# Attention's first chunk of queries and keys loaded in the front stage, into a place of its own

## The reference, cut to what matters

```python
x = x + gnn(layernorm(x), adj)            # 16 heads of 32, adjacency mask
h = rmsnorm(layernorm(x), g1)
q, k, v = split(h @ w_qkv)                # 16 heads of 32; rope on q and k
scores = where(causal, q @ k.T / sqrt(32), -inf)
y = softmax(scores) @ v                   # S = 2048 here
x = x + y @ w_o ; x = x + moe(rmsnorm(x, g2))
```

## Time and profile before

| | us |
|---|---|
| median of 3 runs (lowest, highest) | 2302.75 (2296.74, 2306.21) |
| the profiled execution's own time | 2302.54 |
| span of the profiled execution | 2300.5 |
| what lies around the span | 2.04 |
| front stage, about 702 to 963.1 in the trace | 261 |
| attention stage, 963.1 to about 1735 | 772 |

### The profile page before, as it was taken

How to read it: one execution, slowest core, us unless ns; L and a number is a source line. 1 busy time by engine, 2 the same in 40 slices (tenths; PEclk the granted TensorE clock), 3 DMA queues, 4 the chain that set the end, 5 groups by cost and what they waited for, 6 DMA issues and landing times. The chain is left out here.

```text
span 2300.5 us, 42173 instructions
## 1 busy us (share of the span) xinstructions
PE 2068.8 (90%) x17684; PEld 1222.4 (53%) x17684; DVE 1549.1 (67%) x2552; ACT 1086.7 (47%) x1074; POOL 583.6 (25%) x435
## 2 busy tenths in 40 slices
PE   6899999999995999799999999999991699999997
PEld 3444444444442444344444444444471688888886
DVE  6689999999985567668768777776346544444441
ACT  4778898898971333213444444444420222222221
POOL 2510000000001012414545545544320222222211
PEclk9999999999997999859999999999975799999999
DMA  6421221211215012542030030011030444444421
GB/s 238 147 82 52 73 68 55 73 68 54 74 31 192 37 46 101 162 96 50 19 88 24 24 86 26 20 38 46 24 137 37 170 106 118 120 120 119 119 60 23
DMA packets 86759, 185.33 MB, mean 81 GB/s; under 512 B 13900, under 2 KB 23116, under 8 KB 81036
## 3 DMA queue, kind: packets, MB, share of 16 engines
q1 hardware_dynamic: 77612, 161.68, 21.6%
q0 software_dynamic: 8960, 20.98, 5.0%
HBM read 137.68 MB, written 40.49 MB: 77 GB/s over the span
## 5 line engine op out<-in xcount | busy, mean ns | idle before, releaser
L1406 DVE TENSOR_REDUCE t_rm<-t_m 128x1 f32<-128x512 f32 (+3 forms) x640 | 373.3, 606 | 161.2 <-PE t_m L1527 96.5
L1336 ACT ACTIVATE t_E<-t_s 128x1024 f32<-128x1024 f32 (+3 forms) x320 | 277.3, 895 | 419.8 <-PE t_s L1544 219.4
L1283 POOL TENSOR_TENSOR t_total<-t_E 128x1024 f32<-128x1024 f32 (+2 forms) x151 | 291.8, 1944 | 217.2 <-PE t_d L1571 211.5
L543 ACT ACTIVATE m_step<-m_ub,gat_bias 128x2048 bf16<-128x2048 f32 x128 | 250.0, 1989 | 17.4 <-DMA m_ub<-scratch_uac 12.0
L685 PE MATMUL m_bd<-m_mask,m_S 128*32 128x512 bf16 x3072 | 230.4, 379 | 12.2 <-DVE m_mask L633 12.1
L685 PE MATMUL m_bd<-gat_adjT,m_S 128*32 128x512 bf16 x2496 | 201.4, 379 | 4.9 <-PE m_dn L685 4.9
L685 PE MATMUL m_bd<-m_mask,m_neg 128*32 128x512 bf16 x2496 | 189.0, 379 | 0.0
L1527 PE MATMUL t_m<-tq_K,tq_Q 96*128 96x512 f32 (+2 forms) x320 | 143.7, 477 | 34.4 <-DMA tq_K<-scratch_parts 15.8
L1909 POOL DMA_INDIRECT out<-e_ye,e_token x40 | 80.9, 2024 | 350.9 <-DVE e_ye L2011 341.5
L2075 PE MATMUL e_h<-e_xTh,e_w1h 128*128 128x320 f32 x512 | 159.9, 312 | 3.6 <-PE e_y L2094 2.2
L855 POOL TENSOR_TENSOR o_wq<-o_wq,o_gcol 128x2048 f32<-128x2048 f32 x3 | 11.3, 3807 | 590.3 <-DMA o_wq<-in_L_ffn_w_qkv 590.3
(11 more groups left out here) (317 smaller groups left out, 4126.9 us busy)
## 6 DMA issues: line engine op xcount, KB each, us to landing
a_adj<-in_adj SPq DMA_DIRECT2D x16, 1024.0 KB, 4.9
m_ub<-scratch_uac SPq DMA_DIRECT2D x16, 1024.0 KB, 5.0
e_w1r<-in_L_ffn_w SPq DMA_DIRECT2D x8, 2048.0 KB, 9.4
e_w2r<-in_L_ffn_w SPq DMA_DIRECT2D x8, 2048.0 KB, 9.0
tq_Q<-scratch_parts SPq DMA_DIRECT2D x48, 256.0 KB, 4.9
gat_scale<-scratch_uac SPq DMA_DIRECT2D x32, 256.0 KB
scratch_parts<-o_hi SPq DMA_DIRECT2D x32, 256.0 KB, 2.2
scratch_parts<-o_lo SPq DMA_DIRECT2D x32, 256.0 KB, 2.7
```

The source lines that it names most:

```text
L543: act.activation(step(n), ub[h % 2][:, :].rearrange("p (t q) -> p t q", t=T), ACT.Relu, bias=bias[:, j, h:h + 1], scale=BIG).then_inc(step ...
L1283: pool.tensor_tensor(total[:, two, off:BANK], E[a % 3][:, two, off:BANK], E[(a + 1) % 3][:, two, off:BANK], ALU.add).then_inc(summed[z], 1)
L1336: act.activation(E[n % 3][:, two, off:BANK], ps_s[:, two, off:BANK], ACT.Exp, scale=SCALE).then_inc(exp_done[z], 1)
L1406: dve.tensor_reduce(rm[:, h, t, ch:ch + 1], ps_m[i % 2][:, 0:w], AX, ALU.max).then_inc(entry_read, 1)
```

## The change

Chunk 0 of Q and K of the first four heads gets tensors of its own (`Q0`, `K0`), allocated ahead of the front stage. The front stage's SP loads them (`load_first`) between the stores of qk job 11 and those of job 12, after a wait that three even jobs be stored. The triangles, the block of ones and the ones of K's chunk 0 are made by the front stage's POOL at its start, ahead of `pool.wait_ge(g_in, ...)`. The attention stage drops these instructions and starts SP with chunk 1. The semaphores that count these loads and the setup are the same by name in both stages, with no clearing between them.

For this Q, K, `late_rows` and `late` are now lists of chunks [partition, head, 512], of which chunk 0 is the separate tensor. All accesses are rewritten for that. `load_k` thereby becomes 12 loads of 256 KB where it was three of 1 MB, with rows of 2 KB where they were of 8 KB, in each of its three calls. The ones are written in seven pieces of 2048 in the attention stage where there were two of 8192, and one in the front.

In `ORDER` the v jobs 13, 14 and 15, which stood among the qk jobs 14 to 31, now stand behind the last of them.

```diff
@@ -772,7 +772,7 @@
     ORDER += turns(1) + outs(10, 11) + [qk[3], vs[4]] + outs(11, 12) + [qk[4], vs[5]] + outs(12, 13)
     ORDER += [("var", 2), ("norm", 2), qk[5], vs[6]] + outs(13, 14) + [qk[6], vs[7]] + turns(2) + outs(14, 15)
     ORDER += [qk[7], vs[8]] + outs(15, 16) + [qk[8], vs[9], ("var", 3), ("norm", 3), qk[9], vs[10], qk[10], vs[11]]
-    ORDER += turns(3) + qk[11:14] + [vs[12]] + qk[14:19] + [vs[13]] + qk[19:25] + [vs[14]] + qk[25:] + [vs[15]]
+    ORDER += turns(3) + qk[11:14] + [vs[12]] + qk[14:] + vs[13:]
...
@@ -829,7 +829,17 @@
                 sp.dma_start(C[:, :], cos).then_inc(cs_in, 16)
                 sp.dma_start(S[:, :], sin).then_inc(cs_in, 16)
                 load_x(3)
+
+                def load_first():
+                    sp.wait_ge(sent[0], 32 * 3)
+                    rows = lambda part: parts_dram[part, 0:P, 0:BANK].rearrange("(g d) n -> d g n", g=4)
+                    for stack, order, arrived in ((keep["Q0"], (0, 0, 1), keep["q_in"]), (keep["K0"], (2, 3, 2), keep["k_in"])):
+                        for b, part in enumerate(order):
+                            sp.dma_start(stack[b * DH:(b + 1) * DH, :, :].bitcast(F32), rows(part)).then_inc(arrived, 16)
+
                 for n, (m, g, c) in enumerate(QK):
+                    if n == 12:
+                        load_first()
                     sp.wait_ge(parts_ready, n + 1)
                     for z, part in enumerate((hi, lo)):
                         sp.dma_start(parts_dram[2 * m + z, g * P:(g + 1) * P, c * BANK:(c + 1) * BANK],
@@ -847,6 +857,19 @@
                     pool.tensor_tensor(spun[n % 2][:, :], raw[n % 2][:, :], C[:, c * BANK:(c + 1) * BANK],
                                        ALU.mult).then_inc(cos_done, 1)
...
+
+                triq, trik, ones, setup = (keep[n] for n in ("triq", "trik", "ones", "setup"))
+                pool.memset(triq[:, :], 0.0).then_inc(setup, 1)
+                pool.memset(trik[:, :], 0.0).then_inc(setup, 1)
+                pool.memset(ones[:, :], 1.0).then_inc(setup, 1)
+                pool.wait_ge(setup, 3)
+                pool.affine_select(out=triq[:, :], in_=triq[:, :], compare_op=ALU.is_ge, fill=-1e30,
+                                   base=0, pattern=[[-1, P]], channel_multiplier=1).then_inc(setup, 1)
+                pool.affine_select(out=trik[:, :], in_=trik[:, :], compare_op=ALU.is_ge, fill=-1e30,
+                                   base=0, pattern=[[1, P]], channel_multiplier=-1).then_inc(setup, 1)
+                pool.wait_ge(setup, 5)
+                pool.memset(keep["K0"][ROWS:ROWS + 1, :, :].bitcast(F32), 1.0).then_inc(keep["k_ones"], 1)
+                pool.wait_ge(keep["k_ones"], 1)
 
...
@@ -1092,13 +1115,16 @@
 
 
         with Stage(nc, "tq") as places:
-            Q, K0 = places.sb("Q", [P, G, N], F32R), places.sb("K0", [P, G, N], F32R)
-        late_rows, late = st.sb("rows", [P, G, N]), st.sb("late", [P, G, N])
-        K = [K0, st.sb("K1", [P, G, N], F32R)]
+            Qs, K0s = (places.sb(n, [P, NC - 1, G, BANK], F32R) for n in ("Q", "K0"))
+        rowss, lates = (st.sb(n, [P, NC - 1, G, BANK]) for n in ("rows", "late"))
+        K1s = st.sb("K1", [P, NC, G, BANK], F32R)
+        chunks = lambda first, others: [first[:, :, :]] + [others[:, c, :, :] for c in range(NC - 1)]
+
+        Q, late_rows, late = chunks(keep["Q0"], Qs), chunks(keep["rows0"], rowss), chunks(keep["late0"], lates)
+        K = [chunks(keep["K0"], K0s), [K1s[:, c, :, :] for c in range(NC)]]
...
         E = [st.sb(f"E{i}", [P, G, BANK]) for i in range(3)]
         total = st.sb("total", [P, G, BANK])
-        ones = st.sb("ones", [P, DH])
-        triq, trik = st.sb("triq", [P, P], BF16), st.sb("trik", [P, P], BF16)
+        triq, trik, ones = (keep[n] for n in ("triq", "trik", "ones"))
...
         ve, lg = keep["inv"][:, 1, :], prob
-        W = late[:, 3, :].rearrange("p (k n) -> p k n", k=KD)
-        oT = [late[:, i, :].rearrange("p (k n) -> p k n", k=KD) for i in range(3)]
-        row = lambda t: late_rows[:, t % 4, t // 4 * BANK:(t // 4 + 1) * BANK]
+        W, oT = late[3], late[0:3]
+        row = lambda t: late_rows[t // 4][:, t % 4, :]
...
@@ -1152,25 +1177,27 @@
                 def load_k(q):
                     if q >= 2:
                         sp.wait_ge(s_full[1], (q - 1) * NS)
-                    for b, part in enumerate((2, 3, 2)):
-                        sp.dma_start(K[q % 2][b * DH:(b + 1) * DH, :, :].bitcast(F32), rows(q, part)).then_inc(k_in[q % 2], 16)
+                    for c in range(NC):
+                        for b, part in enumerate((2, 3, 2)):
+                            sp.dma_start(K[q % 2][c][b * DH:(b + 1) * DH].bitcast(F32),
+                                         rows(q, part, slice(c * BANK, (c + 1) * BANK))).then_inc(k_in[q % 2], 16)
 
...
@@ -1201,9 +1228,8 @@
                     for k in range(KD):
                         sp.dma_start(gcol[:, k:k + 1], g2[k * P:(k + 1) * P].rearrange("(p o) -> p o", o=1)).then_inc(g_in, 16)
 
-                for c in range(2):
-                    load_q(0, c)
-                    load_k_first(c)
+                load_q(0, 1)
+                load_k_first(1)
                 maxima(0, 0)
                 for c in range(2, NC):
                     load_q(0, c)
...
@@ -1247,24 +1273,17 @@
                     sp.wait_ge(res_ready, 4 * c + 4)
                     sp.dma_start(rv[:, some, :], X1[:, some, :]).then_inc(res_out, 16)
                     sp.wait_ge(z_ready, 4 * c + 4)
-                    sp.dma_start(zv[:, some, :], late_rows[:, :, c * BANK:(c + 1) * BANK]).then_inc(z_out, 16)
+                    sp.dma_start(zv[:, some, :], late_rows[c]).then_inc(z_out, 16)
...
             @block.gpsimd
             def _(pool):
-                pool.memset(triq[:, :], 0.0).then_inc(setup, 1)
-                pool.memset(trik[:, :], 0.0).then_inc(setup, 1)
-                pool.memset(ones[:, :], 1.0).then_inc(setup, 1)
-                pool.wait_ge(setup, 3)
-                pool.affine_select(out=triq[:, :], in_=triq[:, :], compare_op=ALU.is_ge, fill=BIG,
-                                   base=0, pattern=[[-1, P]], channel_multiplier=1).then_inc(setup, 1)
-                pool.affine_select(out=trik[:, :], in_=trik[:, :], compare_op=ALU.is_ge, fill=BIG,
-                                   base=0, pattern=[[1, P]], channel_multiplier=-1).then_inc(setup, 1)
-                pool.wait_ge(setup, 5)
                 for r in range(2):
-                    pool.memset(K[r][ROWS:K1, :, :].bitcast(F32), 1.0).then_inc(k_ones[r], 1)
-                    pool.wait_ge(k_ones[r], 1)
+                    for c in range(1 - r, NC):
+                        pool.memset(K[r][c][ROWS:K1].bitcast(F32), 1.0).then_inc(k_ones[r], 1)
+                    pool.wait_ge(k_ones[r], NC)
+
                 def add_row(t):
                     pool.wait_ge(y_ready, t + 1)
                     pool.tensor_tensor(X1[:, t, :], X1[:, t, :], row(t), ALU.add).then_inc(res_ready, 1)
...
@@ -1520,12 +1539,12 @@
                         if q == 0:
                             pe.wait_ge(k_first[c], 48)
                         elif c == 0:
-                            pe.wait_ge(k_in[q % 2], 48 * ((q + 1) // 2))
+                            pe.wait_ge(k_in[q % 2], 48 * NC * ((q + 1) // 2))
                     if n >= 2:
                         pe.wait_ge(entry_read, n - 1)
                     diag = ch == c
-                    mm = pe.matmul(ps_m[i % 2][:, 0:w], Q[0:ROWS, h, t * P:(t + 1) * P],
-                                   K[q % 2][0:ROWS, h, ch * BANK:ch * BANK + w], start=True, stop=not diag)
+                    mm = pe.matmul(ps_m[i % 2][:, 0:w], Q[c][0:ROWS, h, t % 4 * P:(t % 4 + 1) * P],
+                                   K[q % 2][ch][0:ROWS, h, 0:w], start=True, stop=not diag)
...
@@ -1536,13 +1555,13 @@
                     if s == BEGIN[c] and z == 0:
                         pe.wait_ge(m_in[c], 64 * (q + 1))
                         if c == 0 and q < 2:
-                            pe.wait_ge(k_ones[q], 1)
+                            pe.wait_ge(k_ones[q], NC)
...
                     for h in (2 * z, 2 * z + 1):
-                        mm = pe.matmul(ps_s[:, h, off:BANK], K[q % 2][0:K1, h, kt * P:(kt + 1) * P],
-                                       Q[0:K1, h, c * BANK + off:(c + 1) * BANK], start=True, stop=not diag)
+                        mm = pe.matmul(ps_s[:, h, off:BANK], K[q % 2][kt // 4][0:K1, h, kt % 4 * P:(kt % 4 + 1) * P],
+                                       Q[c][0:K1, h, off:BANK], start=True, stop=not diag)
...
@@ -2168,6 +2187,14 @@
                     stage_masks(nc, sem, keep, scratch["uac"], scratch["near"], scratch["inv"])
                 recycle()
                 keep["X1"], keep["prob"] = k.sb("X1", [P, T, D]), k.sb("prob", [P, T, EXPERTS])
+
+                with Stage(nc, "first") as first:
```

(12 more changed lines are left out.)

## The result

| | us |
|---|---|
| after, median of 18 runs (lowest, highest) | 2291.11 (2281.67, 2301.77) |
| before, median of 18 runs beside them | 2301.59 (2292.35, 2308.44) |
| ratio after / before, 95% interval | 0.9967 [0.9954, 0.9979] |
| profiled execution: time, span | 2290.23, 2288.5 |

The ratio is 7.6 us in 2301.6 (4.8 to 10.6), the medians differ by 10.5. The forecast was 15.2: half to two thirds of it came. By its interval the gain lies within 0.5%.

What follows compares the result with a forecast made beforehand. PE was taken to bound the kernel, busy 2068.8 of 2300.5 us, with time to win at the seam before attention, where it stood 15.77 us. Terms 4.4 + 10.0 + 0.8 = 15.2 gave 2287.3 us, range 2278 to 2298.

Steps and rivals of the forecast that it cites:

- Part 1: Front stage's end: with the v jobs moved last, the last store lands earlier and attention starts sooner; gain 4.4 us.
- Part 2: Seam to attention: chunk 0 is loaded early, so PE starts 0.2 us after the barrier; gain 10.0 us.
- Part 3: Start of attention: chunk 1's loads arrive without a wait, and some entries run at the upper clock; gain 0.8 us.
- Part 4: Everything behind: later attention moves along unchanged, and POOL's setup and the extra load issues cost 0.
- A: Attention's entries: gain as summed, clock falls soon after they start and rises at the same place of work; 2287.3 us, chance 0.62.
- B: Attention's entries: the clock stays up because PE no longer stands long; 2272.7 us, chance 0.10.
- C: Attention's first quad: the clock rises later in the work, with two misses; 2295.3 us, chance 0.18.
- D: Attention's first quad: the clock stays down through most of it, 2340 us if up to the second K load; chance 0.05.
- E: PE's start in attention: another wait replaces that for the loads, so only the stage's end is won; 2298.1 us, chance 0.05.
- class "same": Whole kernel: a time within about 0.5%, 11.5 us, of no change; chance 0.23.

Runs made afterwards that it cites:

- order_only: The kernel before with only the changed `ORDER`, no early loads: 2300.02 us, ratio 0.9973 to the kernel before.
- loads_at_job8: The changed kernel with the six early loads issued before the store of job 8 instead of job 12: 2288.62 us, ratio 0.9919.
- k_in_pieces: The kernel before with each `load_k` issued as 12 loads of 256 KB: 2297.94 us, ratio 0.9986.
- fill_one: loads_at_job8 with one unread 128 by 128 float32 product behind each of the first 49 entries of the first quad, turns excepted: 2271.34 us, ratio 0.9868.
- pool_one_job_later: The changed kernel with POOL's cosine product waiting for the rotation of the job before it: 2281.82 us, ratio 0.9912.

## Why the forecast was right in direction and too high

**Part 1 (forecast 4.4).** As a term of its own it was right: order_only 4.6. In the changed kernel it came to -0.7 (start - E 6.22 against 5.56). The step that failed stands in part 1 and part 2 together. Part 1 said that "a longer run at the same rate adds nothing", with under 2 us if DVE fell behind by 0.1 per job. DVE fell behind by 3.77 - 3.43 = 0.34 per job. Part 2 had the cause in hand: it put the landing of job 12's store near 895 and let ACT stand for 2 us, once, costed at 0 because PE has three free banks. The store landed at 895.32 in a front that ran some 2 us ahead of the trace before, so 2.4 us later than put there, and the stall was 4.45; PE indeed lost nothing, and the 0 was wrong all the same: the end of the stage waits for the last store, not for PE, and the v jobs that had given DVE room to catch up were just what the change took away. Two of the forecast's own signs show it: PE's gap at the seam was 6.41 us where it named about 1.5, and the first SP issue of attention came at 961.68 where it named 958.7, though the front's products ended 2 us earlier. Each edit was weighed against the kernel before, not against the kernel with the other edit in it.

**Part 2 (forecast 10.0).** Right: the wait behind the barrier fell from 10.22 to 0.19, which is 10.0, and 9.9 in both kernels with the old order.

**Part 3 (forecast 0.8).** It came to nothing in the changed kernel, since PE stood 6.4 us instead of 1.4 and the clock was down when it started (12.03 us for the entries against 12.15). No wait for chunk 1, as said. The brief rise at 998 to 1000 then gave 1.7 that was not forecast (maxima 0 are 9.4 earlier, maxima 1 11.1). In loads_at_job8, where PE stood 1.15, a few entries ran at full clock: the term's mechanism, though its size can't be told apart from the rest.

**Part 4 (forecast 0).** Right by k_in_pieces, and POOL's pieces of ones were done at 967.03 + 7.04 = 974.07 with no one waiting.

**The sum, closed.** In the profiled executions PE's last product of the front came 2.06 earlier and maxima 1 then 11.1 earlier relative to it, together 13.2; the time of these two executions differs by 12.3. What lies behind maxima 1 scatters: from there to the last store of the attention stage it is 712.3 us before, 713.5 after, and 703.9 to 716.7 in the kernels of the table, with dips of the clock at changing places. So single executions can't carry a difference of 5 us here, and the table counts within one trace.

**The cases.** A's outcome held, low clock from the entries on and a rise in the same place of the work, behind the first denominators (about 1014 in after and 1017 in loads_at_job8, against 1026). Its premise, a clock still up when the entries start, was met only in loads_at_job8; in the changed kernel it fell at 959 to 960, in the longer gap. B's price came close in fill_one (2272.7 forecast, 2271.3 measured; maxima 1 are 25.0 us earlier behind E than before), but only added products brought it about. The Trainium skill, page "TensorE: Matmul & The Clock Gate", section on oscillation in real kernels, asks for a PE without idle gaps. In loads_at_job8 the gap fell to 1.15 us and the clock fell just the same; but PE also stood 0.20 to 0.26 us four times for DVE in the first 4 us of entries, so only the long gap is ruled out as the cause. C, D and E did not come in the changed kernel's trace. The median, 2291.1, lies in the range of 2278 to 2298, in its upper half. That is in part luck: the range reached that far for C and E, and the loss came by neither, but by a stall costed at 0, of which the unforeseen rise of the clock gave 1.7 us back. Also, the gain of 7.6 by the ratio falls in the class "same", to which the forecast gave 0.23, and not in "faster" with its 0.72.

## What to carry to other kernels

Cost a delay by who ends the stage, not by the bottleneck engine: a stall that PE's buffers swallow can still arrive at the last store. When a change has two parts, cost each with the other in place; slack that one spends may be what the other removes. And put early loads into a queue where the stores behind them have slack, not merely where their data is ready: four jobs earlier brought the next stage's start 5.3 us nearer (6.22 against 0.96) and maxima 1 3.8 us. The whole kernel gained 2.5 us by the medians and 11 by the two ratios, so its size there is not settled.

## What the hardware showed that I had not expected

**DVE and POOL on two-operand products.** DVE's sine product takes 0.69 us alone, 1.09 beside the last part of POOL's product and 1.75 beside all of it. In the last case it ends at 938.99 + 1.75 = 940.74 and POOL's at 938.93 + 1.27 = 940.20, as if DVE's had hardly moved while POOL's ran. In the second it ends at 889.33 and POOL's at 888.78: 0.55 behind POOL's again. DVE's sum, met in the same way, takes 1.64 for 0.69. The shuffle, with one operand, keeps its 0.73 in either case. Where DVE is first, as at 903.02 in pool_one_job_later, DVE keeps its 0.68 and POOL's product stretches from 1.27 to 1.59. The Trainium skill, page "GPSIMD Engine Reference", section on specifications, says that the two share their SBUF interfaces, with contention for DVE instructions that read two SBUF inputs; the trace agrees, and adds the price.

**A rhythm that locks.** In the changed kernel the slower period, once there, lasts to the end of the run. ACT's eviction of the next job ends within 0.1 us of DVE's shuffle, POOL starts with it, and both products start together, in each of 14 jobs in a row (901 to 950). In these runs two things kept or restored the old period: a job without DVE work, and a wait that keeps the two products apart.

**The clock is held by work.** One unread product behind each entry holds 1.00 through 53 us in which the same entries, with PE standing only 1.15 us ahead of them, ran at 0.50. The product both adds work and fills the short waits for DVE between entries, and no run here tells the two apart.
